# Superslots spread over the first 345 slots of a layer, ScalarE's copies of counts ahead of its one-hots, and the first 24 gathers in the prologue

## The chip, the cores and the metric

One core of one Trainium2 chip runs the whole program in one launch. The metric is the device time of an execution in microseconds, as the median of several runs. TensorE is called PE, VectorE DVE, ScalarE ACT, GpSimd POOL and SyncE SP, as the profile does.

## The reference

Four graph networks are applied one after the other to 3125 nodes with 64 features, over 100000 edges sorted by destination. Each is added to its input: `x = x + net(relu(layernorm(x)))`.

```python
# 1: three layers of attention over the edges (64 features an edge)
q, k, v = x @ Wq + bq, x @ Wk + bk, x @ Wv + bv;  e = edge_attr @ We
alpha = sum(q[dst] * (k[src] + e)) / sqrt(64)
w = softmax of alpha over the edges of each dst
x = segment_sum((v[src] + e) * w, dst) + x @ Ws + bs   # then relu, and layer norm after layers 1 and 2
# 2: ten steps  h = 0.9 * norm * segment_sum((h * norm)[src], dst) + 0.1 * feat
# 3: segment_sum(norm * (concat(x[src], edge_attr_32) @ weight), dst) + bias
# 4: attention by sums el[src] + er[dst] of projected nodes, softmax over dst, weighted sum
```

Networks 2 and 4 of the kernel work on a dense matrix that holds how many edges lead from each node to each other node. So the edges have to be counted into that matrix, and this is done beside the three attention layers of network 1.

## The kernel before, in words

**Slots and batches.** The edges of a block of 128 destinations are cut into slots of 128 edges, one edge on each partition. Two slots (`BT`) make a batch, and there are 415 batches (`NBAT`) in each of the three layers (`conv(l)`, l = 0, 1, 2). Batches lie in eleven windows: eight of 45, then 30, 15 and 10 (`WIN_BATCHES`). A softmax is made at the end of each window. While window w is expanded and its logits are made, window w - 1 is weighted and summed; `steps(w)` interleaves the two.

**The work of a batch j** is spread over the engines, each of which has its order written out, tied by semaphores:

- POOL issues two indirect DMAs (line 617), which gather the source rows of the node table into a ring, `RING`, of 110 slots (55 batches). Batch j may be gathered once the aggregation of batch j - 55 is done (`slot_free`, semaphore `bmm`).
- SP loads the edge features of the batch into the same ring slots (line 635), with the same wait.
- ACT makes the one-hots of destinations (`one_hot_rows`, lines 668 and 671) four batches ahead from broadcast rows that it loads itself, and sums the products (`sum_products`, line 681), which gives the logits.
- PE expands the queries to the edges (`expand`, line 761), and aggregates for window w - 1 (`aggregate`, line 772).
- DVE multiplies expanded queries and gathered rows (`product`, line 890), makes the weighted one-hots (`weighted`, line 919) and adds the aggregates (`add`, line 932).
- For the first 196 batches (`HIST`) of layers 0 and 1, DVE and PE also count sources (`sources`, lines 898 and 899; `count_sources`, line 784), for the degrees.

**Superslots.** The 595 superslots of 256 edges, which fill the matrix of edge counts, are shared out: 245, 245 and 105 of them (`ADJ_N`) go to the three layers. `adjacency_slots(l, j)` says which superslots go with batch j. For a superslot, DVE makes three one-hots (`key_hots`, lines 906 and 908), PE multiplies them and adds what earlier superslots left in the same strip (`window_counts`, lines 798 and 800, in one PSUM tile `WPS`), ACT copies the tile out (`copy_counts`, line 689) and stores it to memory (`store_counts`, line 700). PE may write `WPS` again only after ACT's copy (semaphore `acp`), and ACT issues a store only after the store before it has landed (semaphore `kst`), since neighbouring strips may be the same. In `adjacency_slots` of before, the first 196 batches weigh 36 each and later ones up to batch 411 weigh 100 each (layers 0 and 1); in the last layer all 411 weigh the same.

ACT's order for each batch j is the following.

```python
for k in adjacency_slots(l, j - 3) if j >= 3 else ():
    store_counts(k)
if j + 4 < NBAT:
    one_hot_rows(j + 4)
for k in adjacency_slots(l, j - 2) if j >= 2 else ():
    copy_counts(k)
sum_products(j)
```

**The prologue** (the first phase) finds out which edges are in which slots, by gathers on POOL (lines 336 and 342) and a long chain on DVE. It writes the normalised nodes to the node table (line 297), and makes `IDX`, the source of each edge of each slot, by transposes on PE (line 388) and a copy out of PSUM (line 511). `IDX` is what the layers gather by. A barrier of all engines stands between the prologue and the first layer. In it, each layer first projects all nodes (lines 743 to 880), which takes some 30 us before the first product.

Of the kernel before, what the change touches and what calls it, by code (L numbers as in the profile page):

```python
# [4 lines left out]
N, E, D, D32, L = 3125, 100000, 64, 32, 3  # L5
# [3 lines left out]
BT = 2  # L9
# [16 lines left out]
NBAT = sum(WIN_BATCHES)  # L26
ROWS = NBAT * BT
WIN_T0 = [BT * sum(WIN_BATCHES[:w]) for w in range(len(WIN_BATCHES))]
WIN_N = [BT * n for n in WIN_BATCHES]
NWIN = len(WIN_BATCHES)  # L30
# [4 lines left out]
RW = 162  # L35
# [4 lines left out]
REGS = 5  # L40
HIST = NC // 4
STEPS, TELE = 10, 0.1
EPS = 1e-5
# [59 lines left out]
def adjacency_slots(l, j):  # L103

    light, last = 196, NBAT - 4
    weigh = lambda k: 36 * min(k, light) + 100 * max(0, k - light) if l < 2 else k
    return share_weighed(ADJ_N[l], weigh(min(j, last)), weigh(min(j + 1, last)), weigh(last))
# [20 lines left out]
def build(nc, a, out):  # L128
# [9 lines left out]
    with ctx:  # L138
# [74 lines left out]
        def cols(w):  # L213

            o = WIN_T0[w]
            return o if w < 5 else 512 + o - WIN_T0[5]
# [26 lines left out]

        tmp = Words(layer_mem, LOW + 3225)
        with phase(nc, "qp ldd ldx ldw lds cst cio cnt gi ms p1 p2 p3 p4 c1 c2 c3 c4 mm mc st var std h row tr key ktr kc wr") as (block, s):
            FD = V(tmp.take(NG), NG, dt=i32)
# [34 lines left out]
            @block.sync  # L281
            def _(sp):
                sp.dma_start(FD, a["first_dst"].rearrange("(o n) -> o n", o=1).to_broadcast([P, NG])).then_inc(s["ldd"], 16)
                sp.dma_start(F4, a["first_dst4"].rearrange("(o n) -> o n", o=1).to_broadcast([P, NG4])).then_inc(s["ldd"], 16)
                sp.dma_start(X0, blk(x_d)).then_inc(s["ldx"], 16)
                sp.dma_start(SRT, a["src_t"]).then_inc(s["lds"], 16)
                sp.dma_start(MQ[0:D], a["w_edge_key"]).then_inc(s["ldw"], 16)
                sp.dma_start(WQT[0:D], a["w_query_t"]).then_inc(s["ldw"], 16)
                for l in range(L):
                    sp.dma_start(WU[l][0:D + 1, AB:UW], a["w_skip"][l]).then_inc(s["ldw"], 16)  # L290
                sp.dma_start(WVE, a["w_edge_value"]).then_inc(s["ldw"], 16)
                sp.dma_start(BV, a["L0_gnn_bv"].rearrange("(o l) n -> o l n", o=1).to_broadcast([P, L, D])).then_inc(s["ldw"], 16)
                for q, n in ((0, "ln_gamma"), (1, "ln_beta")):
                    sp.dma_start(GB[:, :, q, :], a["L0_gnn_" + n].rearrange("(o l) n -> o l n", o=1).to_broadcast([P, L - 1, D]))\
                        .then_inc(s["ldw"], 16)
                sp.wait_ge(s["h"], 1)
                sp.dma_start(blk(xt_t), H[:, :, 0:D]).then_inc(s["wr"], 16)
                sp.wait_ge(s["c1"], 1)
                for to, fr in ((crow, CI), (brow, BI), (flag_row, FI)):
                    sp.dma_start(to, fr).then_inc(s["wr"], 16)  # L300
                sp.wait_ge(s["row"], 1)
                sp.dma_start(row_t[0:WIN_T0[8], :].rearrange("(w p) e -> p w e", w=8), DB[0:WMAX, 0:8]).then_inc(s["wr"], 16)
                for w in range(8, NWIN):
                    sp.dma_start(row_t[WIN_T0[w]:WIN_T0[w] + WIN_N[w], :], DB[0:WIN_N[w], w]).then_inc(s["wr"], 16)
                sp.wait_ge(s["ldw"], 16 * 9)
                sp.wait_ge(s["wr"], 16 * 8)

            @block.gpsimd
            def _(pool):
# [30 lines left out]
                for fr, to in ((dst_d, D4), (src_d, S4)):  # L340
                    for w in range(NQ):
                        pool.indirect_dma_start(
                            out=to[0:Q4, w], out_offset=None, in_=fr.rearrange("(g e) -> g e", e=G4 * P),
                            in_offset=bass.IndirectOffsetOnAxis(ap=GI4[0:Q4, w:w + 1], axis=0)).then_inc(rec4, 16)

            @block.scalar
# [9 lines left out]
            def _(pe):  # L356
# [12 lines left out]
                for w in range(NQ):  # L369
                    ins = pe.matmul(ps[0:1, cols4(w):cols4(w) + Q4], CNT4[0:Q4, w:w + 1], identf[0:Q4, 0:Q4],  # L370
                                    start=True, stop=True)
                ins.then_inc(s["p1"], 1)
                pe.wait_ge(s["c2"], 1)
                for q, e in ((0, 0), (1, P - 1)):
# [3 lines left out]
                ins.then_inc(s["p2"], 1)  # L378
                pe.wait_ge(s["c1"], 1)
                pe.wait_ge(s["c3"], 1)  # L380
# [3 lines left out]
                pe.matmul(ps[:, 1024:1024 + NWIN], ONES[0:1, :], DZ[0:1, :, 0], start=True, stop=True).then_inc(s["p3"], 1)  # L384
                pe.wait_ge(s["c4"], 1)
                for w in range(NWIN):
                    n = WIN_N[w]
                    ins = pe.transpose(ps[:, 1536 + cols(w):1536 + cols(w) + n], SF[0:n, w], identf[0:n, 0:n])
                ins.then_inc(s["p4"], 1)
                pe.wait_ge(s["key"], 1)  # L390
# [8 lines left out]
            def _(dve):  # L399
# [67 lines left out]

                dve.wait_ge(rec, 16 * 2 * NWIN)
                st.link(dve.tensor_copy(DF, DG))
                dve.sem_inc(s["c2"], 1)  # L470
# [9 lines left out]
                dve.sem_inc(s["row"], 1)  # L480
                st.link(dve.tensor_copy(SF, SG))
                dve.tensor_scalar(MK, DZ, 0.5, -BIG, ALU.is_lt, ALU.mult)
# [12 lines left out]
                st.link(ins)  # L495
                dve.sem_inc(s["c4"], 1)
                st.link(dve.tensor_tensor(WH, FR, LR, ALU.not_equal))
# [8 lines left out]
                for k, o, n in ((0, 0, WIN_T0[5]), (512, WIN_T0[5], ROWS - WIN_T0[5])):  # L506
                    dve.tensor_copy(DZT[:, o:o + n], ps[:, k:k + n])
                dve.tensor_scalar(OH0, ps[:, 1024:1024 + NWIN], pid1, None, ALU.is_equal)
                dve.wait_ge(s["p4"], 1)
                for k, o, n in ((0, 0, WIN_T0[5]), (512, WIN_T0[5], ROWS - WIN_T0[5])):  # L510
                    ins = dve.tensor_copy(IDX[:, o:o + n], ps[:, 1536 + k:1536 + k + n])
                st.link(ins)

# [20 lines left out]
        def conv(l):  # L534
# [6 lines left out]
            h_mem = Words(high.at, LOW + HIGH)  # L541
            RING = V(m.take(R_SLOTS * RW), R_SLOTS, RW)
            U = V(m.take(NB * AB), NB, AB)
# [58 lines left out]
            with phase(nc, names) as (block, s):  # L602
# [9 lines left out]
                def _(pool):  # L612
                    st = Steps(pool, s["pst"])
                    for j in range(NBAT):
                        slot_free(pool, j)
# [29 lines left out]
                def _(act):  # L645
# [59 lines left out]
                    for w in range(NWIN):  # L705
                        for ja, jb in steps(w):
                            for j in ja:
                                for k in adjacency_slots(l, j - 3) if j >= 3 else ():
                                    store_counts(k)
                                if j + 4 < NBAT:  # L710
                                    one_hot_rows(j + 4)
                                for k in adjacency_slots(l, j - 2) if j >= 2 else ():
                                    copy_counts(k)
                                sum_products(j)
# [960 lines left out]
```

## Time and profile before

| | |
|---|---|
| median of 3 runs | 4728.33 us (4718.66 to 4733.19) |
| profiled execution, its own time | 4739.01 us |
| its span, first to last instruction | 4737.2 us |
| mean granted TensorE clock | 0.804 of full speed |
| busy: PE / DVE / ACT / POOL | 73% / 68% / 51% / 53% |
| first product of layers 0, 1, 2 at | 127.2 / 1305.4 / 2496.7 us |
| last product of layers 0, 1, 2 at | 1214.0 / 2404.6 / 3570.1 us |

Times within the profile count from the first instruction. A share of busy time is a mean over the whole span: the three layers end near 3600 us, and POOL has almost nothing to do after them. "Idle before" is what an engine did not work just before an instruction, and the name behind it is who ended that. A product is an instruction of line 890; there is one for each batch, so that the starts of products tell how a layer moves on.

### The profile page before, as it was taken

The numbers are of one execution on the slowest core, as the hardware profiler recorded it, in microseconds if no ns is written. First come the engines' busy times: TensorE is split into PE (matmuls) and PEld (weight loads), VectorE is DVE, ScalarE is ACT, GpSimd is POOL, SyncE is SP. The second block draws the span as 40 slices with busy tenths as digits, with TensorE's granted clock in tenths as the row PEclk, the third lists the DMA queues.
The fourth block names the chain that finished last, engine by engine and source line by source line (L and its number), as shares of the span: only waits on it lengthen the run. The fifth ranks groups of instructions, "written<-read, shape, count | busy, mean of one in ns | idle before, by whom it ended". The sixth has DMA issues, their size and how long they took to land. (4 is left out here: it accounts for less than half of the span.)

```text
span 4737.2 us, 91072 instructions
## 1 busy us (share of the span) xinstructions
PE 3467.0 (73%) x24128; PEld 3021.0 (64%) x24128; DVE 3241.6 (68%) x10295; ACT 2428.0 (51%) x8514; POOL 2505.3 (53%) x2592
## 2 busy tenths in 40 slices
PE   3666666667667676666666877777775799997789
PEld 2555545555555565555555776677775799996788
DVE  7577767777667776677764787777785333354998
ACT  0766667666276666667527666666542000000555
POOL 5777777776277777677617777777742000000000
PEclk9788888888677878788866788888775899997555
DMA  3444445444244444444414444444423200000000
GB/s 78 99 102 106 103 113 122 118 120 104 56 99 96 107 104 116 112 116 122 106 49 100 100 108 103 106 99 109 99 57 130 68 2 2 2 2 1 2 3 3
DMA packets 576845, 384.28 MB, mean 81 GB/s; under 512 B 421913, under 2 KB 498833, under 8 KB 576343
## 3 DMA queue, kind: packets, MB, share of 16 engines
q1 hardware_dynamic: 373463, 151.17, 12.5%
q0 software_dynamic: 81344, 84.68, 10.3%
q10 hardware_dynamic: 121536, 142.57, 10.1%
q8 instruction: 213, 3.49, 0.3%
q14 instruction: 289, 2.37, 0.2%
HBM read 312.87 MB, written 65.24 MB: 80 GB/s over the span
## 5 line engine op out<-in xcount | busy, mean ns | idle before, releaser
L617 POOL DMA_INDIRECT arena<-node_table,arena x1660 | 1605.5, 967 | 605.2 <-issue 470.5
L772 PE MATMUL ps<-arena 128*128 128x129 f32 x4980 | 947.0, 321 | 183.5 <-DVE arena L922 103.5
L681 ACT ACTIVATE arena<-arena 128x129 f32<-128x129 f32 x2490 | 742.8, 301 | 464.4 <-DVE arena L890 457.4
L772 PEld LDWEIGHTS ps<-arena 128*128 128x128 f32 x4980 | 790.3, 226 | 268.6 <-DVE arena L922 138.0
L919 DVE TENSOR_SCALAR arena<-arena 128x128 f32<-128x128 uint16 x2490 | 885.9, 362 | 89.4 <-PE ps L772 40.0
L617 POOL DMA_INDIRECT arena<-last_node_table,arena x830 | 793.1, 955 | 283.2 <-issue 235.1
L890 DVE TENSOR_TENSOR arena<-ps,arena 128x258 f32<-128x258 f32 x1245 | 524.6, 421 | 598.5 <-PE ps L761 238.0
L1198 PE MATMUL ps<-arena 128*128 128x192 bf16 x6875 | 586.6, 247 | 8.1 <-issue 7.1
L1198 PEld LDWEIGHTS ps<-arena 128*128 128x128 bf16 x6875 | 584.7, 98 | 10.1 <-issue 5.6
L761 PE MATMUL ps<-arena 128*128 x2496 | 502.2, 334 | 104.8 <-ACT e L671 35.5
L761 PE MATMUL ps<-arena,e 128*128 x2484 | 495.6, 331 | 96.5 <-DVE arena L890 44.0
L798 PE MATMUL ps<-stage,al 128*128 128x400 bf16 x1190 | 354.3, 385 | 272.9 <-ACT al L689 124.6
L761 PEld LDWEIGHTS ps<-arena 128*128 128x128 f32 x2496 | 421.9, 232 | 172.4 <-issue 155.3
L761 PEld LDWEIGHTS ps<-arena,e 128*128 128x128 f32 x2484 | 411.0, 228 | 164.4 <-issue 145.6
L681 ACT ACTIVATION_READ_ACCUMULATOR arena<-arena 128x1 f32 x2490 | 468.3, 188 | 0.0
L932 DVE TENSOR_TENSOR arena<-arena,ps 128x129 f32 (+1 forms) x1245 | 363.8, 292 | 112.7 <-issue 48.7
L668 ACT ACTIVATE arena<-arena 128x256 f32<-128x256 bf16 x624 | 313.2, 502 | 140.4 <-PE ps L761 47.7
L668 ACT ACTIVATE e<-arena 128x256 f32<-128x256 bf16 x621 | 310.4, 500 | 114.2 <-PE ps L761 41.3
L1479 POOL TENSOR_TENSOR stage<-stage 128x1600 f32<-128x1600 f32 x1 | 3.6, 3551 | 669.4 <-DMA stage<-in_L_gnn_bias 669.4
L908 DVE TENSOR_SCALAR stage<-arena 128x400 bf16<-128x400 uint16 x1190 | 342.9, 329 | 0.0
L1530 PE MATMUL ps<-arena 128*128 128x65 f32 x1250 | 288.8, 419 | 34.5 <-DVE arena L1600 34.4
L1530 PEld LDWEIGHTS ps<-arena 128*128 128x128 f32 x1250 | 272.4, 328 | 51.6 <-DVE arena L1600 50.8
(332 smaller groups left out, 4625.9 us busy)
## 6 DMA issues: line engine op xcount, KB each, us to landing
arena<-in_attr SPq DMA_DIRECT2D x1245, 96.0 KB, 2.2
arena<-slot_rows ACTq DMA_DIRECT2D x249, 320.0 KB
edge_counts<-al ACTq DMA_DIRECT2D x397, 100.0 KB
arena<-node_table,arena POOLq DMA_INDIRECT x1660
edge_counts<-stage ACTq DMA_DIRECT2D x198, 100.0 KB
arena<-last_node_table,arena POOLq DMA_INDIRECT x830
arena<-edge_counts SPq DMA_DIRECT2D x24, 500.0 KB
stage<-edge_counts SPq DMA_DIRECT2D x16, 500.0 KB
```

What stands on the lines that cost most here:

```text
L617: pool.indirect_dma_start(out=RING[:, t % R_SLOTS, XO:XO + XG], out_offset=None, in_=table[:, :], in_offset=bass.IndirectOffsetOnAxis(ap=I ...
L668: act.activation(o, ROWB[r % 2][:, (j % 5) * BT * P:(j % 5 + 1) * BT * P], ACT.Square, bias=pid1, scale=-1.0)\
L681: ins = act.activation(PR[j % 3][:, q], PR[j % 3][:, q], ACT.Copy, accum_out=AL[w % 2][:, c:c + 1])
L761: ins = pe.matmul(UPS[j % 2][:, q * AB:(q + 1) * AB], OHT[j % 6][:, q * P:(q + 1) * P], U[:, bass.ds(b, 1), :].rearrange("p a b -> p (a b) ...
L772: ins = pe.matmul(BPS[j % 2][:, 0:AB], WOH[j % 2][:, q], RING[:, r + q, D32:D32 + AB], start=q == 0, stop=q == BT - 1)
L798: ins = pe.matmul(WPS, LOH[k % 3][:, q], KOH[k % 3][q], start=q == 0, stop=t == 0 and q == G4 - 1)
L890: dve.tensor_tensor(PR[j % 3], UPS[j % 2].rearrange("p (a b) -> p a b", b=AB), RING[:, r:r + BT, D32:D32 + AB], ALU.mult).then_inc(s["pr"], 1)
L908: ins = dve.tensor_scalar(KOH[k % 3][q], iota1[:, 0:NB * WIN], KEY4[:, adj0 + k, q:q + 1], None, ALU.is_equal)
L919: ins = dve.tensor_scalar(WOH[j % 2][:, q], iota1[:, 0:P], DZT[:, t:t + 1], PT[w % 2][:, c:c + 1], ALU.is_equal, ALU.mult)
L932: dve.tensor_tensor(to, to, BPS[j % 2], ALU.add).then_inc(s["add"], 1)
L1198: last = pe.matmul(ps[:, o + 256 * c:o + 256 * c + 3 * D], adj3[:, sx, bass.ds((d0 + c) * P, P)], g3[:, sx].rearrange("p a b -> p (a b)"), ...
L1530: ins = pe.matmul(EOS[i % 2][:, c * (D + 1):(c + 1) * (D + 1)], XB[t % 2][:, c * P:(c + 1) * P], Z[:, sx], start=sx == 0 and c == 0, stop= ...
```

## The change

Three things are changed together.

1. `adjacency_slots` ends at batch 345 (`NBAT - 70`) instead of 411 in all layers. In layers 0 and 1, batches up to 196 weigh 1 and later ones weigh 2.
2. ACT's order for a batch is now: copy of counts, one-hots, store of counts, row sums.
3. The first 12 batches of layer 0 (`AHEAD`, 24 gathers) are gathered by POOL at the end of the prologue, behind the prologue's own gathers. For this `IDX` is made earlier: DVE copies the sources first, PE transposes them first, and DVE copies `IDX` out of PSUM as soon as it has made and copied `DZ`. A semaphore `ix` says that `IDX` is there, and `xt` that the node table has been written. The temporaries of the prologue start behind the ring's first 24 slots. PE's transposes of `DZ` wait for `ix`, since the indices were in the same part of PSUM.

```diff
+AHEAD = 12
 def adjacency_slots(l, j):
-    light, last = 196, NBAT - 4
-    weigh = lambda k: 36 * min(k, light) + 100 * max(0, k - light) if l < 2 else k
+    light, last = 196, NBAT - 70
+    weigh = lambda k: min(k, light) + 2 * max(0, k - light) if l < 2 else k
     return share_weighed(ADJ_N[l], weigh(min(j, last)), weigh(min(j + 1, last)), weigh(last))
...
+        RING = V(layer_mem, R_SLOTS, RW)
+        tmp = Words(layer_mem + AHEAD * BT * RW, LOW + 3225)
...
                 sp.wait_ge(s["h"], 1)
-                sp.dma_start(blk(xt_t), H[:, :, 0:D]).then_inc(s["wr"], 16)
+                sp.dma_start(blk(xt_t), H[:, :, 0:D]).then_inc(s["xt"], 16)
...
-                sp.wait_ge(s["wr"], 16 * 8)
+                sp.wait_ge(s["wr"], 16 * 7)
+                sp.wait_ge(s["xt"], 16)
...
+                pool.wait_ge(s["xt"], 16)
+                pool.wait_ge(s["ix"], 1)
+                for t in range(BT * AHEAD):
+                    pool.indirect_dma_start(
+                        out=RING[:, t, XO:XO + D], out_offset=None, in_=xt_t[:, :],
+                        in_offset=bass.IndirectOffsetOnAxis(ap=IDX[:, t:t + 1], axis=0)).then_inc(got[t // BT], 16)
...
+                pe.wait_ge(s["c1"], 1)
+                pe.wait_ge(s["c4"], 1)
+                for w in range(NWIN):
+                    n = WIN_N[w]
+                    ins = pe.transpose(ps[:, cols(w):cols(w) + n], SF[0:n, w], identf[0:n, 0:n])
+                ins.then_inc(s["p4"], 1)
                 pe.wait_ge(s["c2"], 1)
...
-                pe.wait_ge(s["c1"], 1)
+                pe.wait_ge(s["ix"], 1)
                 pe.wait_ge(s["c3"], 1)
...
-                pe.wait_ge(s["c4"], 1)
-                for w in range(NWIN):
-                    n = WIN_N[w]
-                    ins = pe.transpose(ps[:, 1536 + cols(w):1536 + cols(w) + n], SF[0:n, w], identf[0:n, 0:n])
-                ins.then_inc(s["p4"], 1)
...
                 dve.wait_ge(rec, 16 * 2 * NWIN)
+                st.link(dve.tensor_copy(SF, SG))
+                dve.sem_inc(s["c4"], 1)
                 st.link(dve.tensor_copy(DF, DG))
...
                 dve.sem_inc(s["row"], 1)
-                st.link(dve.tensor_copy(SF, SG))
+                dve.wait_ge(s["p4"], 1)
+                for k, o, n in ((0, 0, WIN_T0[5]), (512, WIN_T0[5], ROWS - WIN_T0[5])):
+                    ins = dve.tensor_copy(IDX[:, o:o + n], ps[:, k:k + n])
+                st.link(ins)
+                dve.sem_inc(s["ix"], 1)
...
-                dve.wait_ge(s["p4"], 1)
-                for k, o, n in ((0, 0, WIN_T0[5]), (512, WIN_T0[5], ROWS - WIN_T0[5])):
-                    ins = dve.tensor_copy(IDX[:, o:o + n], ps[:, 1536 + k:1536 + k + n])
-                st.link(ins)
...
-                    for j in range(NBAT):
+                    for j in range(0 if l else AHEAD, NBAT):
                         slot_free(pool, j)
...
                             for j in ja:
-                                for k in adjacency_slots(l, j - 3) if j >= 3 else ():
-                                    store_counts(k)
-                                if j + 4 < NBAT:
-                                    one_hot_rows(j + 4)
                                 for k in adjacency_slots(l, j - 2) if j >= 2 else ():
                                     copy_counts(k)
+                                if j + 4 < NBAT:
+                                    one_hot_rows(j + 4)
+                                for k in adjacency_slots(l, j - 3) if j >= 3 else ():
+                                    store_counts(k)
                                 sum_products(j)
```

## Rows read from the trace of the kernel before

**Rows 1.** The page, costliest group: busy, mean ns | idle before, releaser.

```profile
L617 POOL DMA_INDIRECT arena<-node_table,arena x1660 | 1605.5, 967 | 605.2 <-issue 470.5
```

**Rows 2.** Line 890 (products) in window 1 of layer 0, and its waits (us, times).

```profile
L890 DVE TENSOR_TENSOR arena<-ps,arena x45: 417/426/429, 220.4 to 327.2; 128x258 f32<-128x258 f32 x45
...
  DMA arena<-node_table,arena: 20.4, 22
```

**Rows 3.** Line 617 (gathers) in three stretches: ns min/median/max, first and last start.

```profile
L617 POOL DMA_INDIRECT arena<-node_table,arena x90: 941/947/1173, 96.0 to 209.2; - x90
...
L617 POOL DMA_INDIRECT arena<-node_table,arena x361: 941/947/1645, 209.2 to 669.1; - x181
...
L617 POOL DMA_INDIRECT arena<-last_node_table,arena x632: 940/947/1131, 2576.1 to 3371.2; - x158
```

**Rows 4.** Line 890 in windows 5 and 6 of layers 0 and 1.

```profile
L890 DVE TENSOR_TENSOR arena<-ps,arena x45: 409/425/428, 683.5 to 792.4; 128x258 f32<-128x258 f32 x45
...
L890 DVE TENSOR_TENSOR arena<-ps,arena x45: 410/422/429, 808.2 to 918.5; 128x258 f32<-128x258 f32 x45
...
L890 DVE TENSOR_TENSOR arena<-ps,arena x45: 409/422/429, 1866.4 to 1983.9; 128x258 f32<-128x258 f32 x45
...
L890 DVE TENSOR_TENSOR arena<-ps,arena x45: 410/426/429, 1995.8 to 2103.1; 128x258 f32<-128x258 f32 x45
```

**Rows 5.** Timeline of ACT in window 6 of layer 0: start, length, instruction [idle before].

```profile
874.68 0.49 ACT L689 ACTIVATE al<-ps 128x400 bf16<-128x400 f32 x1
...
875.55 0.19 ACT L681 ACTIVATION_READ_ACCUMULATOR arena<-arena 128x1 f32 x1
876.55 0.34 ACTq L700 DMA_DIRECT2D edge_counts<-al  x1
876.99 0.51 ACT L668 ACTIVATE arena<-arena 128x256 f32<-128x256 bf16 x1 [1.24 <-PE ps L761]
...
877.85 0.49 ACT L689 ACTIVATE al<-ps 128x400 bf16<-128x400 f32 x1
```

**Rows 6.** PE's waits in window 5 of layer 0: us, times, longest.

```profile
PE ps L798 <- ACT al L689: 18.1, 14, 3.6
PE ps L798 <- ACT stage L689: 7.4, 7, 1.9
```

**Rows 7.** Line 890: window 0, its first 28; starts of windows 1, 2 (layers 0, 1).

```profile
L890 DVE TENSOR_TENSOR arena<-ps,arena x45: 412/427/429, 127.2 to 211.8; 128x258 f32<-128x258 f32 x45
...
L890 DVE TENSOR_TENSOR arena<-ps,arena x28: 412/426/429, 127.2 to 173.8; 128x258 f32<-128x258 f32 x28
...
L890 DVE TENSOR_TENSOR arena<-ps,arena x8: 417/420/428, 220.4 to 234.6; 128x258 f32<-128x258 f32 x8
...
L890 DVE TENSOR_TENSOR arena<-ps,arena x12: 410/416/428, 337.4 to 359.3; 128x258 f32<-128x258 f32 x12
...
L890 DVE TENSOR_TENSOR arena<-ps,arena x16: 415/419/428, 1514.9 to 1548.6; 128x258 f32<-128x258 f32 x16
```

**Rows 8.** Line 890, batches 345 to 414 of layers 0, 1, and 360 to 414 of layer 2.

```profile
L890 DVE TENSOR_TENSOR arena<-ps,arena x70: 406/419/428, 1002.8 to 1214.0; 128x258 f32<-128x258 f32 x70
...
L890 DVE TENSOR_TENSOR arena<-ps,arena x70: 408/419/429, 2192.5 to 2404.6; 128x258 f32<-128x258 f32 x70
...
L890 DVE TENSOR_TENSOR arena<-ps,arena x55: 411/418/424, 3385.3 to 3570.1; 128x258 f32<-128x258 f32 x55
```

**Rows 9.** The prologue: gathers of line 342, and rows of the timeline.

```profile
L342 POOL DMA_INDIRECT arena<-in_src,arena x5: 1218/1568/2072, 56.4 to 64.2; - x5
...
33.52 0.37 SPq L297 DMA_DIRECT2D node_table<-arena  x1
...
58.50 0.89 DVE L479 CAST arena<-arena 128x1408 bf16<-128x1408 f32 x1
...
64.19 1.23 POOL L342 DMA_INDIRECT arena<-in_src,arena  x1 [0.30 <-issue]
...
89.20 4.23 PE L395 MATMUL ps<-identf,arena 119*128 119x119 f32 x20 [17.62 <-DVEq L526]
...
92.21 1.98 DVE L531 COPY arena<-ps 128x238 f32<-128x238 f32 x5
```

More of the change, by code:

```diff
@@ L241, in norm_act @@
             act.activation(stat[:, 1], stat[:, 1], ACT.Sqrt).then_inc(s["std"], 1)
-        tmp = Words(layer_mem, LOW + 3225)
-        with phase(nc, "qp ldd ldx ldw lds cst cio cnt gi ms p1 p2 p3 p4 c1 c2 c3 c4 mm mc st var std h row tr key ktr kc wr") as (block, s):
+        RING = V(layer_mem, R_SLOTS, RW)
+        tmp = Words(layer_mem + AHEAD * BT * RW, LOW + 3225)
+        with phase(nc, "qp ldd ldx ldw lds cst cio cnt gi ms p1 p2 p3 p4 c1 c2 c3 c4 mm mc st var std h row tr key ktr kc wr xt ix") as (block, s):
             FD = V(tmp.take(NG), NG, dt=i32)
@@ L495, in _ @@
                 st.link(ins)
-                dve.sem_inc(s["c4"], 1)
                 st.link(dve.tensor_tensor(WH, FR, LR, ALU.not_equal))
@@ L507, in _ @@
                     dve.tensor_copy(DZT[:, o:o + n], ps[:, k:k + n])
-                dve.tensor_scalar(OH0, ps[:, 1024:1024 + NWIN], pid1, None, ALU.is_equal)
-                dve.wait_ge(s["p4"], 1)
-                for k, o, n in ((0, 0, WIN_T0[5]), (512, WIN_T0[5], ROWS - WIN_T0[5])):
-                    ins = dve.tensor_copy(IDX[:, o:o + n], ps[:, 1536 + k:1536 + k + n])
-                st.link(ins)
+                st.link(dve.tensor_scalar(OH0, ps[:, 1024:1024 + NWIN], pid1, None, ALU.is_equal))
                 dve.wait_ge(rec4, 16 * 2 * NQ)
@@ L541, in conv @@
             h_mem = Words(high.at, LOW + HIGH)
-            RING = V(m.take(R_SLOTS * RW), R_SLOTS, RW)
+            m.take(R_SLOTS * RW)
             U = V(m.take(NB * AB), NB, AB)
@@ L707, in _ @@
                             for j in ja:
+                                for k in adjacency_slots(l, j - 2) if j >= 2 else ():
+                                    copy_counts(k)
+                                if j + 4 < NBAT:
+                                    one_hot_rows(j + 4)
                                 for k in adjacency_slots(l, j - 3) if j >= 3 else ():
                                     store_counts(k)
-                                if j + 4 < NBAT:
-                                    one_hot_rows(j + 4)
-                                for k in adjacency_slots(l, j - 2) if j >= 2 else ():
-                                    copy_counts(k)
                                 sum_products(j)
```

## The prediction

> **What bounds the kernel now.** The page shows no engine busy above 73% of the span (the table ahead), so the limit has to be looked for stage by stage. Its costliest group is the gathers on POOL [rows 1]: 967 ns of work each, and 605.2 / 1660 = 0.36 us of idle time before one, nearly all of it its own issue. I then asked for the products of DVE (line 890, one per batch) window by window, because their starts are the clock of a layer.
>
> In window 1 of the first layer 45 products run from 220.4 to 327.2, and DVE waited 22 times, 20.4 us in all, for a gather to land [rows 2]. POOL in that time issues without a stop: 361 gathers from 209.2 to 669.1, that is 1.277 us each or 2.55 us a batch; in the last layer 632 gathers take 1.260 us each [rows 3]. So windows 0 to 4 are set by POOL. In windows 5 and 6 it is another matter: there a batch takes 2.48, 2.51, 2.67 and 2.44 us (four windows of two layers, last start minus first over 44) [rows 4], mean 2.52, with 0.858 superslots a batch. The timeline of ScalarE shows why: copy at 874.68, two row sums until 875.74, then nothing until the store at 876.55, which waits for the store before it to land, then the one-hots at 876.99 and the next copy at 877.85: 3.2 us from copy to copy [rows 5]. And PE waits for that copy: 18.1 and 7.4 us in window 5 [rows 6]. So heavy windows are set by ScalarE's serial work and its stores.
>
> With few superslots compute is quicker than POOL. While gathers were still ahead, batches of windows 1 and 2 took 14.2 us for 7, 21.9 for 11 and 33.7 for 15, together 2.11 us a batch; in window 0, without aggregation, 46.6 us for 27, 1.73 [rows 7]. These have 0.309 superslots a batch.
>
> **Superslots, layers 0 and 1.** From the weights of `adjacency_slots`: before, 36/28556 x 245 = 0.309 a batch for 196 batches and 0.858 up to 411. After, 245/494 = 0.496 for 196 batches, 0.992 for 149 batches up to 345, none behind. Price of one superslot: from 2.11 to 2.52 us over 0.549 superslots is 0.75 us, a lower end, since the light batches also count sources. From ScalarE's own row: copy 0.38 and about 0.8 of waiting for the store, 1.14 us [rows 5], the upper end. I take 1.0, between them.
>
> *First 196 batches*: +37 superslots, 8 a window. That work lies beside the 20.4 us that DVE waits for gathers in a window [rows 2]: the pace becomes 2.11 + 0.19 = 2.30, still under 2.55. Cost nothing; if the cover were gone, 37 us a layer.
>
> *Batches 196 to 344*: 149 x 0.134 = +20 superslots where ScalarE sets the pace: +20 us a layer (15 to 23); the pace goes from 2.52 to 2.65.
>
> *Batches 345 to 414*: 57 superslots leave. Now the 70 products take 1214.0 - 1002.8 = 211.2 us and 2404.6 - 2192.5 = 212.1 us [rows 8]. Without the superslots compute needs 211 - 57 = 154 us. But POOL comes next: it can be only some 8 batches ahead there (110 slots hold 55 batches, 45 of them wait for aggregation), so 62 batches x 2.53 = 157 us plus 3 us of landing = 160 us. The gathers set it: -51 and -52 us. Sum: -31 and -32 us.
>
> **Superslots, last layer.** 105 over 345 instead of 411 batches: 0.304 instead of 0.255. Windows 0 to 7 are gather-bound at 1.26 us [rows 3], cost nothing. Windows 8 to 10 lose 14; their 55 products take 184.8 us [rows 8] with POOL long ahead. There each superslot is some 0.8 us of DVE and PE: -11 us (0 to -14).
>
> **Gathers in the prologue.** POOL's last prologue gather starts at 64.19 and takes 1.23, then POOL idles until 96.0 [rows 3, 9]. 24 gathers at 1.25 us would end at 95.7, beside DVE's last copies (92.21 + 1.98). But next to DVE's long operations POOL is slower: five of those gathers took 1.22 to 2.07 us, median 1.57 [rows 9]. I take 1.25 + 0.26, so POOL ends at about 102 and the layer begins 7 us late (0 to 16). DVE's own order changes without a new stall: the copy of the sources goes ahead of line 469's, PE turns them while DVE still makes DZ, and the indices are ready at about 61.4 (58.50, where the copy to bf16 starts now, + 0.89 for the copy of the sources put ahead, + 0.9 for this one, + 1.1 for two copies out of PSUM), before POOL asks for them at 65.7. PE's transposes of DZ now wait for the indices, because they use the same PSUM; behind them on PE stands only the work for the keys, which starts at 89.20 [rows 9]. The table goes to memory at 33.52 on SP's queue [rows 9], long before; SP's last wait is only split in two, and nothing is queued behind it. DVE does the same instructions, so it ends at 94.2 as now, and POOL's end is what is late next.
>
> What does the head start give? The first product moves from 127.2 to 134. Window 0 had 45 products in 84.6 us and at its own pace needs 44 x (1.73 + 0.1) = 81, so it ends near 215 instead of 211.8, and window 1 starts at 224 instead of 220.4 [rows 2, 7]. Gathers stand at 24 when the layer begins, so POOL reaches slot 110 at 103 + 86 x 1.25 = 211 and must wait for the first aggregation of window 1, near 227. Batch 55 is then gathered at 229.5; before it was at 209.2 + 22 x 1.28 = 237.4 [rows 3]. The head start of 24 x 1.25 = 30 us shrinks to 8 us (0 to 19, the upper end if POOL is not slowed and window 0 keeps 1.73), because the ring is full. From there the layer follows POOL, so -8 us.
>
> SP's loads of edge features are not moved: they begin with the layer, as now, some 30 us ahead of the first product, so they hold nothing up.
>
> **A rule.** The rows say that prologue gathers lengthen next to DVE [rows 9]. If every one of the 24 took the median of 1.57 us and 0.30 of issue, 24 x 1.87 = 45 us, POOL would end at 111, the layer would start 15 us late and the head start would be gone: 0 instead of -8, inside the forecast's own range. The Trainium skill, SBUF — State Buffer, "Who interferes with whom", holds that GpSimd cannot write its descriptors at all while a copy, cast or tensor_scalar of VectorE runs in a two-port mode. By it the longer time is the nearer one. The trace agrees that they lengthen; by how much is open.
>
> **ScalarE's order.** Copies ahead of the one-hots: the same instructions, two queues of consequence behind them. PE gets its accumulator back 0.86 us sooner (one-hot pair, 876.99 to 877.85 [rows 5]), the one-hots have four batches of slack, and the store now waits ahead of the row sums instead of ahead of the one-hots; what is queued behind it are the sums, for which DVE's products wait three batches later. But in heavy windows it is ScalarE that never rests, and its sum of work and store waits is unchanged. Worth nothing (0 to -25 us a heavy window if PE's waits of [rows 6] really end something).
>
> **Sum.** -31 - 32 - 11 - 8 = -82 us. The profiled execution took 4739.0 us (span 4737.2), so 4657 us; the median of the runs is 4728.3, 10.7 less, so **4646 us**.
>
> **Rivals.**
> *The reordering frees the heavy windows.* For it: PE's 25.5 us of waiting on copies in window 5 [rows 6]. Against: ScalarE has no slack. Then POOL bounds all: in layer 0 batch 414 lands at 229.5 + 360 x 2.53 + 3 = 1143 instead of 1214.0, -71; layer 1 without the head start -63; last layer -11. Total -145: 4583.
> *Stores take back half.* Nearly every batch now has a store, and its landing varies. At a heavy pace of 2.80 instead of 2.65: 298 x 0.15 = +45, total -37: 4691.
> *Slower: the store chain becomes the bound.* A store is issued only when the last has landed; 3.2 us lie from one copy to the next in [rows 5]. At 0.99 stores a batch the pace is then the chain's. It decides from (82 + 14)/298 = 0.32 us a batch, a pace of 2.97. At 3.05 it gives 298 x 0.40 - 82 = +37: 4765. Against: mean distance of stores in windows 5 and 6 is 2.52/0.858 = 2.94, and that holds ScalarE's work in batches without one.
> *No change*: only between these two.
>
> **Numbers.** 0.3% is 14 us, about what a measurement can tell from no change. Forecast (4620 to 4680) 0.57; freed (down to 4570) 0.17; half (4680 to 4714) 0.15; within 0.3% 0.04; slower 0.07. So faster 0.89. The range 4600 to 4705 leaves out half of the second case and the last two.
>
> **What would show it.** Products of batches 345 to 414 in about 160 us with DVE waiting for gathers in windows 8 to 10; heavy windows near 2.65 us a batch; window 1 to 3 unchanged in length; POOL idle near 15 us before gather 111 of the first layer; the first product near 134; the last layer's tail 11 us shorter. Wrong would be heavy windows at 2.5 (too high a forecast) or at 2.9 and above, or windows 1 to 3 longer than before.

## The result and the profile after

The changed kernel took 4744.0 us (median of four runs, 4740.1 to 4748.2) against 4723.6 us for the kernel before on the same chip: a ratio of 1.0036, 95% interval 1.002 to 1.0053. It is slower by some 20 us, where the forecast was 82 us faster; the time lies outside the range.

The profiled execution took 4740.11 us (span 4738.3). That of before, 4739.01, was 15 us above the median of its neighbours here, so a subtraction of the two traces shows only 1 of the 20 us. It still shows where the time went. In the changed kernel the products stand in line 901, the gathers in 628 (351 in the prologue), row sums in 692, copies in 700, stores in 711, one-hots in 679 and 682.

A row of products gives the instruction, its count, the shortest, median and longest in ns, and the first and last start in us. The products of the first layer: window 0; window 1; batches 180 to 344, with what DVE waited for ahead of them; windows 5 and 6; batches 345 to 414. Then batches 180 to 344 and 345 to 414 of the second layer, and 360 to 414 of the last. Columns as in [rows 2].

```profile
L901 DVE TENSOR_TENSOR arena<-ps,arena x45: 410/427/429, 138.8 to 229.9; 128x258 f32<-128x258 f32 x45
...
L901 DVE TENSOR_TENSOR arena<-ps,arena x45: 406/411/429, 242.5 to 336.1; 128x258 f32<-128x258 f32 x45
...
L901 DVE TENSOR_TENSOR arena<-ps,arena x165: 408/425/428, 581.9 to 1062.2; 128x258 f32<-128x258 f32 x165
its engine sat idle before it (us, times) until:
  PE ps L772: 107.1, 69
...
L901 DVE TENSOR_TENSOR arena<-ps,arena x45: 409/425/428, 702.9 to 826.2; 128x258 f32<-128x258 f32 x45
...
L901 DVE TENSOR_TENSOR arena<-ps,arena x45: 408/426/428, 838.8 to 967.0; 128x258 f32<-128x258 f32 x45
...
L901 DVE TENSOR_TENSOR arena<-ps,arena x70: 411/420/429, 1065.0 to 1229.6; 128x258 f32<-128x258 f32 x70
...
L901 DVE TENSOR_TENSOR arena<-ps,arena x165: 407/426/429, 1761.7 to 2253.3; 128x258 f32<-128x258 f32 x165
...
L901 DVE TENSOR_TENSOR arena<-ps,arena x70: 414/420/429, 2256.3 to 2420.7; 128x258 f32<-128x258 f32 x70
...
L901 DVE TENSOR_TENSOR arena<-ps,arena x55: 411/418/424, 3405.7 to 3570.5; 128x258 f32<-128x258 f32 x55
```

For batches 180 to 344, which [rows 4] cover only in part, the kernel before had these rows (layers 0 and 1):

```profile
L890 DVE TENSOR_TENSOR arena<-ps,arena x165: 409/421/429, 567.4 to 1000.8; 128x258 f32<-128x258 f32 x165
its engine sat idle before it (us, times) until:
  PE ps L761: 65.8, 49
...
L890 DVE TENSOR_TENSOR arena<-ps,arena x165: 409/425/430, 1746.2 to 2189.6; 128x258 f32<-128x258 f32 x165
```

The two layers can be added up stretch by stretch, each from first start to next first start. Layer 0: up to the first product +11.6 (138.8 against 127.2), to window 1 another +10.5, to batch 180 -7.6 (339.4 against 347.0), to batch 345 +47.7 (483.1 against 435.4), to batch 414 -46.6 (164.6 against 211.2). Layer 1: heavy stretch +48.3 (494.6 against 446.3), tail -47.7. In the heavy windows a batch takes 2.80, 2.91, 2.90 and 2.81 us, mean 2.86, where [rows 4] give 2.52. So the tails gave almost what was forecast, and the heavy stretches (batches 180 to 344) and the beginning of the first layer took it all back.

The prologue, and POOL when the ring is full. A row of the timeline is start, length, instruction and the idle time ahead of it.

```profile
100.56 0.94 POOL L351 DMA_INDIRECT arena<-node_table,arena  x1 [0.30 <-issue]
...
107.53 0.94 POOL L628 DMA_INDIRECT arena<-node_table,arena  x1 [6.02 <-POOLq L89]
...
215.34 0.94 POOL L628 DMA_INDIRECT arena<-node_table,arena  x1 [0.30 <-issue]
244.18 1.68 POOL L628 DMA_INDIRECT arena<-node_table,arena  x1 [27.90 <-PE ps L783]
```

POOL's last prologue gather ends at 101.5, as forecast (102), but the layer begins 6.0 us behind it. Later POOL stands 27.9 us before gather 111, where about 15 were forecast.

ScalarE in window 6 of layer 0, two stores and what follows them:

```profile
883.69 0.34 ACTq L711 DMA_DIRECT2D edge_counts<-al  x1
884.07 0.31 ACT L692 ACTIVATE arena<-arena 128x129 f32<-128x129 f32 x1 [1.76 <-DMA edge_counts<-stage]
...
887.95 0.34 ACTq L711 DMA_DIRECT2D edge_counts<-stage  x1
888.34 0.31 ACT L692 ACTIVATE arena<-arena 128x129 f32<-128x129 f32 x1 [0.16 <-issue]
...
888.85 0.19 ACT L692 ACTIVATION_READ_ACCUMULATOR arena<-arena 128x1 f32 x1
891.80 0.50 ACT L700 ACTIVATE al<-ps 128x400 bf16<-128x400 f32 x1 [2.76 <-PE ps L811]
```

The store waits 1.76 us for its predecessor to land, and the row sums stand behind it; then the copy, now directly behind the sums, waits 2.76 us for PE's counts, with one-hots behind it that wait for neither. ScalarE, which the prediction took for the engine without slack, idles.

### The profile page after: what moved, and what is told of

The parts are those of the page before. It is cut to its first block and busy times, and to the rows that moved or that the text cites. A ratio compares the mean times of both kernels' runs of the same rounds, so it can differ in the third digit from the quotient of the medians.

```text
span 4738.3 us, 91075 instructions
## 1 busy us (share of the span) xinstructions
PE 3404.3 (72%) x24128; PEld 2965.6 (63%) x24128; DVE 3236.9 (68%) x10295; ACT 2404.3 (51%) x8514; POOL 2511.6 (53%) x2592
## 5 line engine op out<-in xcount | busy, mean ns | idle before, releaser
L628 POOL DMA_INDIRECT arena<-node_table,arena x1636 | 1581.3, 967 | 686.2 <-issue 449.6
L783 PE MATMUL ps<-arena 128*128 128x129 f32 x4980 | 923.6, 315 | 193.8 <-DVE arena L933 101.6
L783 PEld LDWEIGHTS ps<-arena 128*128 128x128 f32 x4980 | 767.5, 220 | 270.5 <-DVE arena L933 138.2
L772 PE MATMUL ps<-arena 128*128 x2496 | 481.9, 324 | 92.4 <-issue 39.0
L772 PEld LDWEIGHTS ps<-arena 128*128 128x128 f32 x2496 | 404.8, 223 | 160.0 <-issue 142.9
L809 PEld LDWEIGHTS ps<-stage,al 128*128 128x128 bf16 x1190 | 99.4, 111 | 408.9 <-issue 324.9
```

Of the source, the lines that this page charges most:

```text
L628: pool.indirect_dma_start(out=RING[:, t % R_SLOTS, XO:XO + XG], out_offset=None, in_=table[:, :], in_offset=bass.IndirectOffsetOnAxis(ap=I ...
L772: ins = pe.matmul(UPS[j % 2][:, q * AB:(q + 1) * AB], OHT[j % 6][:, q * P:(q + 1) * P], U[:, bass.ds(b, 1), :].rearrange("p a b -> p (a b) ...
L783: ins = pe.matmul(BPS[j % 2][:, 0:AB], WOH[j % 2][:, q], RING[:, r + q, D32:D32 + AB], start=q == 0, stop=q == BT - 1)
L809: ins = pe.matmul(WPS, LOH[k % 3][:, q], KOH[k % 3][q], start=q == 0, stop=t == 0 and q == G4 - 1)
```

## Experiments

ScalarE's order in a batch j is written here with four letters: S the store of counts (slot j-3), O the one-hots (j+4), C the copy (j-2), Σ the row sums. Before it is S O C Σ, in the change C O S Σ. Each ratio is to the kernel before on the same chip; where two kernels ran on different chips, ratios are compared.

**The parts alone, on a slow chip.** Four kernels: the new weights alone, the new order alone, the prologue gathers alone, and all but the order.

```
# e1: kernel before with
-    light, last = 196, NBAT - 4
-    weigh = lambda k: 36 * min(k, light) + 100 * max(0, k - light) if l < 2 else k
+    light, last = 196, NBAT - 70
+    weigh = lambda k: min(k, light) + 2 * max(0, k - light) if l < 2 else k
# e2: kernel before with S O C Σ -> C O S Σ
# e3: kernel before with the change's AHEAD = 12 and all its lines of the prologue
# e4: changed kernel with C O S Σ -> S O C Σ
```

> Only the superslots are spread over 345 slots. Theory A (stores and copies get steeper with density: one superslot in nearly every batch costs more than the 1.0 us that was assumed, whatever the order): windows 5 and 6 of layers 0 and 1 take 2.8 to 2.9 us a batch as in the changed kernel, and with the last layer's gain of 14 us and a tail about 50 us shorter in layers 0 and 1 the time is 4700 to 4725 us. Theory B (the new order on ScalarE does the harm): windows 5 and 6 stay near 2.65 us a batch and the time is near 4650 us.

> Only ScalarE's order is changed. Theory A: the order is worth nothing, windows 5 and 6 stay near 2.52 us a batch, 4724 us within 0.3%. Theory B: the store's wait ahead of the row sums costs 0.15 to 0.3 us a batch in the 219 batches of each of two layers that are not bound by gathers, so the time is 4760 us or more.

> Only the 24 gathers in the prologue. Theory A (the first layer begins 11.6 us late, because POOL needs 6 us from its last gather to the barrier's end, and the full ring gives the head start back): 0 to 12 us slower than before, 4724 to 4736 us. Theory B (the head start still gives 8 us as forecast): 4716 us.

> The changed kernel with ScalarE's old order. Theory A: as the changed kernel, 4744 us within 0.3%, with 2.8 to 2.9 us a batch in windows 5 and 6. Theory B: near 4660 us, with 2.65 us a batch there.

Here the kernel before took 5748.1 us. Measured: spread 1.0013 (1.0 to 1.0026), order 1.0045 (1.0028 to 1.0061), prologue 0.9972 (0.9959 to 0.9986), all but order 0.9979 (0.9966 to 0.9992). The slowness shows on SP's queue, in its loads of edge features. First stands a stretch of the run of the new weights alone on this chip, then the first 55 loads of the kernel before on a usual one:

```profile
L635 SPq DMA_DIRECT2D arena<-in_attr x10: 690/700/709, 117.8 to 157.7; - x10
```

```profile
L635 SPq DMA_DIRECT2D arena<-in_attr x55: 372/373/787, 96.8 to 138.1; - x55
```

In that stretch the loads come 4.4 us apart instead of 0.77, and its first 55 take 160 us instead of 41. DVE's waits for them over the whole run (us, times, longest):

```profile
DVE arena L877 <- DMA arena<-in_attr: 252.1, 8, 40.6
DVE arena L890 <- DMA arena<-in_attr: 243.0, 80, 9.9
DVE arena L919 <- DMA arena<-in_attr: 142.9, 68, 5.6
```

Some 640 us of waiting for these loads can hide much of what the edits do. The four decide nothing about the usual chips, except that the order costs even there. All were repeated on others.

**All but the order; no landing wait; even weights.** e5 is e4's kernel again. e6 is the changed kernel in which a store waits only for the store before the last, and goes to a fixed strip of its buffer instead of one whose address is read from a table (so it leaves out the counts' true places, and the register loads with them). A copy of counts also waits for a landing, that of the store three before it, whose buffer it takes; e6 keeps this wait. e7 is the kernel before with even weights.

```
# e6
-                        if k:
-                            act.wait_ge(s["kst"], 16 * k)
-                        act.dma_start(adj_t[:, bass.ds(wins[0][t - wins[1]], NB * WIN)], ACC[t % 3]).then_inc(s["kst"], 16)
+                        if k >= 2:
+                            act.wait_ge(s[f"kst{k % 2}"], 16 * (k // 2))
+                        o = t % NW4 * NB * WIN
+                        act.dma_start(adj_t[:, o:o + NB * WIN], ACC[t % 3]).then_inc(s[f"kst{k % 2}"], 16)
...
# e7
-    weigh = lambda k: 36 * min(k, light) + 100 * max(0, k - light) if l < 2 else k
+    weigh = lambda k: k
```

> The changed kernel with ScalarE's old order, again, as the first four runs were on a chip on which SP's loads of edge features and no longer POOL's gathers set the pace (the kernel before took 5748 us there). Where the kernel before takes some 4724 us: theory A (density of superslots) gives 4744 us within 0.3% and 2.8 to 2.9 us a batch in windows 5 and 6; theory B (the new order does harm) gives some 4700 us, 0.9% under the changed kernel, and 2.65 to 2.7 us a batch there.

> The changed kernel, but each superslot is stored to a strip fixed in advance and only the store before the last must have landed (counts go to wrong places; strips are then read and used as they are). If the landing of one store before the next is what makes windows 5 and 6 take 2.8 to 2.9 us a batch (theory A1), they fall to 2.5 or less, gathers then set the pace, and the time falls by 40 to 70 us to some 4680 us. If it is the chain of copy, matmul and copy on one PSUM tile, or ScalarE's sum of work (theory A2), they stay at 2.8 and the time stays within 0.3% of 4744 us.

> The kernel before, with the same weight for all 411 batches: 0.596 superslots a batch in layers 0 and 1. If the cost of a superslot rises with density and is hidden below some 0.6 a batch (theory A), windows 1 to 7 all follow the gathers at 2.4 us a batch, the tail is 17 superslots lighter, and the time is 40 to 60 us under before. If a superslot costs the same wherever it lies (rival), the gain of the late windows is lost in windows 1 to 4 and the time is within 0.3% of before.

Measured: e5 4707.7 us, 0.9951 (0.9932 to 0.997); e6 4619.9, 0.9782 (0.976 to 0.9805); e7 4652.2, 0.9842 (0.9824 to 0.986). The old order gives back 0.0085 of the change's 1.0036, some 40 us. Without a store's wait for the one before, the changed kernel falls by 0.0254, 120 us, where 40 to 70 were expected, although every copy, store and superslot is still there. Its products (line 902 there) for batches 180 to 344 of layer 0:

```profile
L902 DVE TENSOR_TENSOR arena<-ps,arena x165: 411/426/440, 572.5 to 992.7; 128x258 f32<-128x258 f32 x165
```

420.2 us against 480.3 for the same 165 batches in the changed kernel, with DVE's wait for PE at 52.2 instead of 107.1. ScalarE still waits for landings, now ahead of the copies; in window 5 (us, times, longest):

```profile
ACT al L699 <- DMA edge_counts<-al: 6.2, 8, 1.1
...
ACT stage L699 <- DMA edge_counts<-stage: 2.5, 4, 1.3
```

With even weights, 0.596 superslots a batch, the stretch is bounded by gathers again (e7, layer 0, with what DVE waited for ahead of the products):

```profile
L890 DVE TENSOR_TENSOR arena<-ps,arena x165: 408/427/435, 579.7 to 985.3; 128x258 f32<-128x258 f32 x165
...
  DMA arena<-node_table,arena: 76.9, 68
  PE ps L761: 19.3, 16
```

**Two orders between, and the parts again.** e8 moves only the copy (S C O Σ), e9 only the store (O C S Σ), in the changed kernel. e10 is e1's kernel, e11 e3's.

```
# e8: the order of the three ahead of sum_products(j)
-  copy_counts(j - 2); one_hot_rows(j + 4); store_counts(j - 3)
+  store_counts(j - 3); copy_counts(j - 2); one_hot_rows(j + 4)
# e9
-  copy_counts(j - 2); one_hot_rows(j + 4); store_counts(j - 3)
+  one_hot_rows(j + 4); copy_counts(j - 2); store_counts(j - 3)
```

> The changed kernel with the order store, copy, one-hots, row sums: the copy is still ahead of the one-hots, but the store and its wait are back at the front. Theory O1 (the harm is the store's wait directly ahead of the row sums): some 0.9951 of before, as with the old order. Theory O2 (the harm is the copy right behind the row sums, where the one-hots no longer cover its wait for PE): some 1.0036 of before, as the changed kernel.

> The changed kernel with the order one-hots, copy, store, row sums: only the store is moved. Theory O1: some 1.0036 of before. Theory O2: some 0.9951 of before.

> Only the superslots are spread, as in the first run of that kind, for a chip on which gathers set the light windows. If the prologue gathers give nothing or cost a little in the run with all but the order (ratio 0.9951), this one has 0.993 to 0.996 of before, with 2.65 to 2.75 us a batch in windows 5 and 6. If the head start is worth the 8 us of the forecast, it has 0.997.

> Only the 24 gathers in the prologue. Theory P1 (the layer begins 11 us late and the full ring eats the head start): within 0.2% of before, window 1 of the first layer starting later than 220.4 us, batch 55 gathered within 5 us of 238. Theory P2 (as forecast): 0.998, with batch 55 gathered at 230.

Measured: e8 4693.9 us, 0.9915 (0.9889 to 0.9941); e9 4714.8, 0.9958 (0.9944 to 0.9972); e10 4697.4, 0.993 (0.9903 to 0.9956); e11 4721.7, 0.9979 (0.9964 to 0.9994). Beside e5's 0.9951, moving the store alone is +0.0007 +- 0.0024 and moving the copy alone -0.0036 +- 0.0032: neither, nor their sum, is the 0.0085 +- 0.0025 of both. The new weights alone (e10), in both layers, at first with DVE's wait for PE:

```profile
L890 DVE TENSOR_TENSOR arena<-ps,arena x165: 410/426/429, 573.1 to 1039.5; 128x258 f32<-128x258 f32 x165
...
  PE ps L761: 96.5, 69
...
L890 DVE TENSOR_TENSOR arena<-ps,arena x70: 411/421/429, 1042.4 to 1204.5; 128x258 f32<-128x258 f32 x70
...
L890 DVE TENSOR_TENSOR arena<-ps,arena x165: 410/426/429, 1736.6 to 2206.0; 128x258 f32<-128x258 f32 x165
...
L890 DVE TENSOR_TENSOR arena<-ps,arena x70: 413/422/429, 2208.5 to 2375.5; 128x258 f32<-128x258 f32 x70
```

Batches 180 to 344 take 469.3 and 471.9 us, +33.9 and +25.6; the tails 162.1 and 167.0, -49.1 and -45.1; the last layer's tail 168.5, -16.3. The prologue alone (e11), window 1 of layer 0:

```profile
L901 DVE TENSOR_TENSOR arena<-ps,arena x45: 415/423/429, 224.9 to 318.1; 128x258 f32<-128x258 f32 x45
```

It starts 4.5 us late but with gathers in hand: batch 55's second gather starts at 227.8 instead of 238.2, and the kernel gains 9 us.

**The order alone, and the landing wait in other company.** e12 is e2's kernel. e13 is e6's edit on e5's kernel, e15 the same edit on the kernel before; both leave out the copy's wait for a landing too. In the old order a copy stands behind the store before it, which has waited for the same landing, so this takes nothing more away; in the new order, where e6 keeps the wait, the copy comes first and can be held up by it. e14 is a version that the runs so far point to.

```
# e14: changed kernel with
-AHEAD = 12
+AHEAD = 6
-    light, last = 196, NBAT - 70
-    weigh = lambda k: min(k, light) + 2 * max(0, k - light) if l < 2 else k
+    light, last = 196, NBAT - 25
+    weigh = lambda k: k
# and the order S C O Σ
```

> Only ScalarE's new order, with the superslots where they were (0.858 a batch in windows 5 and 6), on a chip on which the kernel before takes some 4725 us. Theory O3 (the new order loses time wherever a store has to wait for the landing of the one before, so in proportion to such stores, 74 of 100 here against 87 of 100 in the changed kernel): 1.003 to 1.006 of before, windows 5 and 6 at 2.60 to 2.65 us a batch. Theory O4 (it only hurts at nearly one superslot a batch): within 0.2% of before.

> The changed kernel with ScalarE's old order and with the stores to strips fixed in advance, each waiting only for the store before the last (counts go to wrong places). Theory O3 (the order loses time only together with the wait for landing): as with the new order, 0.978 of before, 2.40 us a batch in windows 5 and 6. Theory O4 (the order costs by itself): 0.970 or less.

> A version meant to beat both: the same weight for 390 batches (0.628 superslots a batch in layers 0 and 1), the order store, copy, one-hots, row sums, and only 6 batches ahead in the prologue. Theory: 0.984 of before from the even spread, 10 us more from a head start of 15 us that costs no later start (POOL is done at 86, before DVE), so 0.980 to 0.982, some 4640 us. Rival: the even spread already follows the gathers and the order adds nothing, 0.984; or the first layer begins late again (POOL's first gather after 100), 0.985.

> The kernel before with the stores to strips fixed in advance, each waiting only for the store before the last (counts go to wrong places). If landing already set windows 5 and 6 of before, they fall from 2.52 to 2.35 us a batch, where gathers set the pace, and the time is 0.985 of before; if ScalarE's own work set them, as the forecast said, they stay at 2.45 or more and the time is within 0.3%.

Measured: e12 4806.2 us, 1.015 (1.0116 to 1.0183); e13 4607.8, 0.9735 (0.9704 to 0.9765); e14 4637.4, 0.9795 (0.9762 to 0.9828); e15 4655.2, 0.9842 (0.981 to 0.9875). e12 was expected at 1.003 to 1.006 at most, and e13 fell between its two theories. The order alone, the term that the forecast put at nothing, costs 73 us. By the traces (4809.1 us against 4737.2) 30 and 21 of them lie in batches 180 to 344 of layers 0 and 1, and 12 in the tail of layer 0. The granted clock in those two stretches was 0.83 in e12 against 0.87 and 0.86 before, and its matmuls were busy 308.7 and 306.9 us instead of 294.6 and 300.4; whether the clock is a cause or a consequence of the longer waits, no run separates. ScalarE's waits in window 5 of layer 0 (us, times, longest), in e12 and then in the kernel before:

```profile
ACT arena L681 <- DMA edge_counts<-al: 11.0, 7, 3.2
ACT arena L681 <- issue: 9.7, 15, 3.9
ACT arena L681 <- DMA edge_counts<-stage: 6.5, 3, 3.5
ACT arena L681 <- DVE arena L890: 4.1, 12, 1.4
ACT stage L689 <- PE ps L800: 3.8, 3, 2.8
```

```profile
ACT e L668 <- PE ps L761: 6.5, 5, 3.3
ACT arena L668 <- DMA edge_counts<-stage: 3.2, 1, 3.2
ACT arena L668 <- DMA edge_counts<-al: 3.1, 3, 1.5
...
ACT e L668 <- DMA edge_counts<-stage: 2.0, 2, 1.4
```

With the same superslots and the same stores, waits that end with a landing go from 10.3 us (five rows, the longest shown) to 17.5, all of them now ahead of the row sums, and waits for DVE's products and for nothing visible appear beside them. Over batches 180 to 344 of the two layers the landing waits go from 24.7 and 32.9 us to 48.8 and 46.6, while ScalarE's work stays (304.4 and 305.2 us before, 302.5 in both layers of e12). In window 5 PE's waits for copies go from 22.9 to 30.4 us. The kernel before without the landing wait (e15, products in line 889), layer 0:

```profile
L889 DVE TENSOR_TENSOR arena<-ps,arena x165: 406/421/430, 568.1 to 974.0; 128x258 f32<-128x258 f32 x165
its engine sat idle before it (us, times) until:
  DMA arena<-node_table,arena: 59.0, 46
  PE ps L760: 16.5, 17
```

405.9 us against 433.4: the same 0.858 superslots a batch, and DVE now waits mostly for gathers. In its windows 5 and 6 a batch takes 2.38, 2.33, 2.31 and 2.34 us, mean 2.34: that is the gathers' pace inside a window. POOL's own is 2.52 a batch [rows 3], so it must have got ahead in the pauses between windows. And e14, layer 0, window 0 and then batches 180 to 344:

```profile
L901 DVE TENSOR_TENSOR arena<-ps,arena x45: 405/425/429, 127.2 to 222.2; 128x258 f32<-128x258 f32 x45
...
L901 DVE TENSOR_TENSOR arena<-ps,arena x165: 406/425/429, 580.4 to 986.6; 128x258 f32<-128x258 f32 x165
its engine sat idle before it (us, times) until:
  DMA arena<-node_table,arena: 59.7, 58
```

With every part of the computation in its place it is 2% ahead of the kernel before, and of the changed one 2.4%.

## Why the prediction was wrong, by its steps

Measured by parts, each against the kernel before on its own chip, the forecast's -82 us comes apart like this: spread -33 (forecast -74), prologue -9 alone (-8) but nothing that the interval can tell from zero on top of the spread, order some +40 (0). With the prologue at -9 that adds to -2, with e5 against e10 (+0.0021 +- 0.0033, 10 us) to +17; the whole measured +20.

**ScalarE's order: worth nothing. This step failed, and it turned the sign.** Alone it costs 73 us, on top of the rest 40. The argument was that ScalarE never rests and that its sum of work and store waits is unchanged by order. Both halves were wrong. Counted from the trace, ScalarE idled 66 and 68 us of the two layers' windows 5 and 6 before, and 92 and 92 after (e5: 80 and 75). And with the order alone (e12) its work was unchanged, but its waits for landings rose from 58 to 95 us over batches 180 to 344 of the two layers. How this comes about is an argument from the code and the timelines: a wait costs only what it is longer than the work that lies between it and its cause. In the old order the one-hots, which have four batches of slack, lie behind the store's wait and ahead of the copy, and the row sums lie between the copy and the next store. In the new one the sums come directly behind the wait for the landing and the copy directly behind the sums, as the two idle times in the timeline of after show. Two simple causes fell: neither the store ahead of the sums (e9) nor the copy ahead of the one-hots (e8) costs the 0.0085 by itself. Only the order in which both meet is dear. The store's place alone does show in one window, window 0 of layer 0: 91.0 us in e9 and 91.1 in the changed kernel, 85.3 and 85.0 in e5 and e8. Whether the cost of the order needs the wait for the landing is not shown: without a store's wait the same swap costs 0.0047 +- 0.0038 (e6 against e13), which is not clear of 0.0085 +- 0.0025. Nor is that pair clean: in e6 the copies still wait 24.1 and 25.3 us for landings in batches 180 to 344 of the two layers, in e13 not at all, and these stretches differ by 15 and 13 us. How the cost divides between the waits for landings, for products and for PE's counts, what the lower clock of e12 has in it, and why the order costs more alone than with the spread, stays open.

**Batches 196 to 344: +20 us a layer.** That the added superslots slow these batches was right, the size not: +34 and +26 with the weights alone, some 1.3 us a superslot (59.5 us for 46 superslots, 3 of each layer's 23 in batches 180 to 195), above the upper end of 1.14. (That upper end is 0.38 for the copy and 0.8 of waiting, which is 1.18, and the row has 0.49 for the copy.) The price was read as ScalarE's work and one wait, as if a superslot cost the same at any density. The transfer records show a chain: in windows 5 and 6 of e10 a store lands 1.83 us (mean) after its issue, and the next is issued 0.65 us (median) behind that; 89% of the stores follow within 1 us on the landing before them, 77% in the kernel before. In [rows 5] too the store at 876.55 comes 0.67 us behind the landing, at 875.88. So a store needs 2.48 us, and 0.992 of them 2.46 us a batch: more than the 2.34 us at which gathers let a batch go inside these windows (e15). At 0.858 it was 2.13, under that pace in the mean; that the kernel before took 2.52 all the same is put down here to stores that come late, which no run tests. The measured pace of e10, 2.70, is also above the chain's 2.46. Taking the wait away gives 120 us in the changed kernel, 102 in e13 against e5 (0.9951 - 0.9735) and 75 in the kernel before. The edit also drops the reading of the address, so some of these sums may be that. [Rows 5] had the chain in view, and the rival of a store chain that becomes the bound named it; its deciding pace of 2.97 was not reached (2.86) and the kernel was slower all the same, because the rival held the other terms fixed, and of these the head start of layer 0 did not come.

**First 196 batches cost nothing: not quite.** In e10 layer 0 needs 6.1 us more up to batch 180 (446.3 against 440.2), layer 1 0.6. With the prologue gathers it was wrong. The head start alone shortened window 0 of layer 0 from 84.6 to 74.1 us (e11); there it is not bounded by POOL, and its superslots, now 22 instead of 14, are paid: 85.3 with the spread (e5), and 91.1 with the new order as well. The forecast allowed 0.1 a batch, 81 in all.

**The tail: -51, -52.** Measured -46.6 and -47.7, in e10 -49.1 and -45.1, with DVE waiting for gathers. Right. The last layer's tail gave -16 to -20 instead of -11. Its first eight windows, held for free, took 894.1 us in both kernels against 888.6 before; but three kernels with the last layer as before (e11, e12, e15) took 891.9 to 893.5 there, so little of the 5.5 us can be the spread's.

**Prologue: POOL ends at about 102, the layer begins 7 us late.** POOL did end at 101.5: the 24 gathers took 35.2 us from first to last start, 1.53 each, where the forecast had 1.51. So the nearer price was the moderate one of the rows, and the rule's 1.87 was not reached:

```profile
L351 POOL DMA_INDIRECT arena<-node_table,arena x24: 940/1016/2158, 65.4 to 100.6; - x24
```

The Trainium skill, SBUF — State Buffer, "Who interferes with whom", would hold a gather back for the whole of a copy, cast or tensor_scalar of VectorE in a two-port mode. The trace does not bear that out as the price of such a run: the median is 1.02 us, and the longest gather, 2.16 us from 80.96 on, lies beside two SCALAR_TENSOR_TENSOR of 1.49 us, which are none of these three. What was missing is a term behind the last gather: 6.02 us until POOL's next, where in the kernel before POOL's first gather came 1.8 us behind DVE's last copy of [rows 9], ended at 94.2. The layer began 11.5 us late and the first product came at 138.8, not 134. Alone the head start is still worth what was forecast, but by two errors that cancel: the first product came 4.8 us later than forecast and window 0 was 6.9 us shorter. With the spread (e5) window 1 starts at 235.3 and batch 55's second gather at 239.0, no earlier than the 236.6 without any head start (e10), and e5 (0.9951) stands no better than e10 (0.993). With the new order too they come at 242.5 and 246.2, where 224 and 229.5 were forecast. With half as many gathers ahead (e14) the first product comes at 127.2 as before.

One reading of the prediction was too strong without harm: of the 605.2 us that POOL idled before gathers, its own issue was 470.5, 78%, and not nearly all.

## What to carry to other kernels

Where a queue waits for each DMA to land before it issues the next, count landing plus issue as a unit in series, and compare the densest stretch with it; spread such work evenly before taking it out of a tail (e7: 77 us faster with nothing but even weights). Reordering the same instructions can cost more than adding some (73 us here), so look at what lies between each wait and its cause, and test a swap of neighbours alone.

A head start in a ring is worth only what the ring's size and the first window's own pace leave of it.

## What the runs showed of the hardware

One chip ran the kernel before in 5748 us instead of 4730, at a mean granted clock of 0.73 to 0.76 instead of 0.80 to 0.81. In e1 on this chip SP's first 55 loads of edge features were issued over 160 us instead of 41; in the stretch shown they took 0.70 us of its queue each instead of 0.37. The cause is not known. Where POOL's gathers ended the prologue (the changed kernel, e5, e11), the first layer's first gather came 6.0 us behind the last of them. Beside SCALAR_TENSOR_TENSOR and TENSOR_TENSOR instructions of DVE gathers of the prologue took up to 2.16 us, beside its copies out of PSUM at 90.6 us and later 0.94. A store of 100 KB from ScalarE landed 1.6 us (median) after its issue, nine in ten within 2.8 (before, e10).
